# A mixture-of-experts layer: slot inversion by DRAM scatters instead of TensorE, an earlier slot computation, sigmoids placed by a table, first expert's tokens mixed in halves

## What is computed

```python
xk = x + (xprev - x) * time_maa_k
xr = x + (xprev - x) * time_maa_r
e_idx = token_ids.reshape(N) * 5099 % 16
pos = (rank of the token among those of its expert)
slot = where(pos < 512, e_idx * 512 + pos, 16 * 512)
expert_in = (xk placed by slot)                     # 16 x 512 x 512
h = square(relu(expert_in[e] @ w_key[e]))           # 512 -> 1024
expert_out = h @ w_value[e]                         # 1024 -> 512
y = expert_out[slot]                                # dropped: zero
out = x + sigmoid(xr @ w_recept.T) * y
```

## Time and profile before

| | us |
|---|---|
| median of 3 runs (lowest, highest) | 886.87 (886.42, 887.04) |
| the profiled execution, its own time | 886.9 |
| its span, first to last instruction | 885.2 |

### The profile page before, as it was taken

One profiled execution on the slowest core, in us unless ns is written; L12 is line 12 of the kernel. 1 busy time (PEld: TensorE's weight loads), 2 busy tenths in 40 slices (PEclk: granted clock), 3 DMA queues, 4 the chain that ended last, 5 costly groups with the idle time before them and its releaser, 6 DMA issues.

```text
span 885.2 us, 10910 instructions
## 1 busy us (share of the span) xinstructions
PE 877.8 (99%) x3920; PEld 723.8 (82%) x3920; DVE 733.0 (83%) x1020; ACT 412.7 (47%) x649; POOL 517.9 (59%) x468
## 2 busy tenths in 40 slices
PE   8999999999999999999999999999999999999997
PEld 6888888888888888888888888888888888888886
DVE  6787856869898989898989898989898988889862
ACT  7765557554444444444343434353535353535350
POOL 2000007677767676767676777677767776772411
PEclk9999999999999999999999999999999999999999
DMA  8765558775748484848484858575757675764521
GB/s 279 278 217 188 192 170 303 245 241 172 279 152 286 141 288 141 296 137 291 144 289 149 280 163 271 167 262 173 260 177 251 190 244 191 237 200 169 175 88 47
DMA packets 74054, 186.41 MB, mean 211 GB/s; under 512 B 11792, under 2 KB 12304, under 8 KB 74000
## 3 DMA queue, kind: packets, MB, share of 16 engines
q1 hardware_dynamic: 46064, 101.67, 35.8%
q0 software_dynamic: 27648, 83.91, 27.5%
q10 hardware_dynamic: 288, 0.13, 0.1%
HBM read 152.11 MB, written 33.55 MB: 210 GB/s over the span
## 4 chain that ended last, share of the span: by engine, by line
PE 98%; issue 1%; DMA 0%; DVE 0%; POOLq 0%; ACT 0%; POOL 0%; ACTq 0%
PE acc L869 32%; PE acc L871 32%; PE acc L870 32%; DMA wr_raw<-w_recept_t 0%; PE acc L885 0%; PE acc L889 0%; PE acc L893 0%; PE rt_bank L931 0%; POOLq L87 0%; POOL out L398 0%; DVE gate L765 0%; DVE xrow L768 0%; ACTq L495 0%; ACT wr_hi L501 0%; ACT xr_hi L507 0%
## 5 line engine op out<-in xcount | busy, mean ns | idle before, releaser
L391 POOL DMA_INDIRECT pair_even<-pairs,row_pair x128 | 140.3, 1096 | 164.2 <-DVE row_pair L704 125.5
L484 ACT ACTIVATE hid<-acc 128x512 f32<-128x512 f32 x128 | 76.6, 599 | 266.0 <-PE acc L871 266.0
L869 PE MATMUL acc<-xk_hi,wk_hi 128*128 128x512 f32 x512 | 199.5, 390 | 0.0
L871 PE MATMUL acc<-xk_hi,wk_lo 128*128 128x512 f32 x512 | 199.5, 390 | 0.0
L870 PE MATMUL acc<-wv_lo,h_hi 128*128 128x512 f32 x512 | 199.3, 389 | 0.0
L871 PE MATMUL acc<-wv_hi,h_lo 128*128 128x512 f32 x512 | 199.3, 389 | 0.0
L869 PE MATMUL acc<-wv_hi,h_hi 128*128 128x512 f32 x512 | 199.3, 389 | 0.0
L870 PE MATMUL acc<-xk_lo,wk_hi 128*128 128x512 f32 x512 | 199.2, 389 | 0.0
L391 POOL DMA_INDIRECT pair_odd<-pairs,row_pair x128 | 138.7, 1083 | 43.8 <-issue 38.7
L398 POOL DMA_INDIRECT out<-xrow,row_tok x64 | 85.7, 1339 | 113.3 <-DVE xrow L768 103.9
L753 DVE TENSOR_TENSOR hid<-hid 128x512 f32<-128x512 f32 x128 | 88.4, 691 | 53.0 <-ACT hid L484 51.3
(11 more groups left out here) (125 smaller groups left out, 1215.3 us busy)
## 6 DMA issues: line engine op xcount, KB each, us to landing
raw<-w_key SPq DMA_DIRECT2D x64, 512.0 KB, 4.6
raw<-w_value SPq DMA_DIRECT2D x64, 512.0 KB, 4.0
gates<-gate SPq DMA_DIRECT2D x64, 256.0 KB, 2.7
xT<-xs_t SPq DMA_DIRECT2D x63, 256.5 KB, 4.2
pair_even<-pairs,row_pair POOLq DMA_INDIRECT x128, 3.2
pair_odd<-pairs,row_pair POOLq DMA_INDIRECT x128, 3.1
xrow<-x,row_tok POOLq DMA_INDIRECT x64, 5.2
gate<-gates,row_tok POOLq DMA_INDIRECT x64, 4.5
```

What stands on the lines that cost most here:

```text
L391: pool.indirect_dma_start(pair[e % 2][:, i, :], None, pairs, bass.IndirectOffsetOnAxis(row_pair[:, a:a + 1], 0)).then_inc(s_pair[e % 2], 16)
L484: act.activation(hid[:, n % H_SLOTS, :], acc[n % 4][:, :], ACT.Relu).then_inc(s_relu, 1)
L869: pe.matmul(bank[:, :], hi, m_hi, start=first, stop=False)
L871: return pe.matmul(bank[:, :], lo, m_hi, start=False, stop=last)
```

## The change

It removes the one-hot matrices, `invert` and `spread`. Instead DVE computes for each token a place in DRAM (`place`); GpSimd waits for it and issues 64 indirect DMAs, each of which scatters 128 token numbers of 4 bytes into the DRAM list `slot_tok`, waits until all have landed, and issues 5 plain DMAs on its own queue: four that load the list, by lanes of 32, into `tok_q`, and one that loads `row_tok`. DVE makes `row_pair` from `tok_q` in round 52. The routing is now 14 pieces in rounds 1 to 19 and 52, its counts on TensorE come after steps 7 and 13, the token ids are loaded earlier on SP, and one strided reduction becomes a contiguous one with a strided write ahead of it. A table places the sigmoids. The first expert's tokens are mixed in 8 pieces of 256 columns in rounds 56 to 63, the first four of them from the first 8 gathers, the rest from the last 8. ACT's table load no longer waits for the identity matrix, which is gone.

```diff
-    PE_COUNT, PE_DROP, PE_INVERT, PE_SPREAD = 12, 22, 41, 44
-    DVE_ROUTE = (6, 8, 14, 16, 18, 19, 24, 25, 26, 28, 29, 30, 32, 33, 34, 36, 37, 42, 45)
-    FIRST_XK = (60, 61, 62, 63)
+    PE_COUNT, PE_DROP = 7, 13
+    DVE_ROUTE = (1, 3, 4, 5, 7, 8, 9, 10, 12, 13, 15, 16, 19, 52)
+    FIRST_XK = (56, 57, 58, 59, 60, 61, 62, 63)
     FIRST_KEY = (46, 49, 52, 55)
+    FIRST_TILE = (0, 1, 1, 1, 1, 2, 3)
+    LATE_TILES = 6
...
@@ sync
+                if k == 1:
+                    sp.dma_start(id_i, ids.rearrange("b (q j) -> (b q) j", j=J)).then_inc(s_ids, 16)
...
@@ gpsimd
+            pool.wait_ge(s_zero, 3)
+            pool.wait_ge(s_place, 1)
+            for j in range(J):
+                pool.indirect_dma_start(slot_tok, bass.IndirectOffsetOnAxis(place[:, j:j + 1], 0),
+                                        tok_id[:, j:j + 1], None).then_inc(s_put[j % 4], 16)
+            for i in range(4):
+                pool.wait_ge(s_put[i], 16 * J // 4)
+            for q in range(Q):
+                lanes = slice(q * BLOCK, (q + 1) * BLOCK)
+                pool.dma_start(tok_q[lanes, :].rearrange("r (b a) -> r b a", b=Q),
+                               slot_tok.rearrange("(b r a) o -> r b (a o)", b=Q, r=BLOCK)).then_inc(s_tok, 16)
+            pool.dma_start(row_tok[:, :], slot_tok.rearrange("(p a) o -> p (a o)", p=P)).then_inc(s_row_tok, 16)
             pool.wait_ge(s_rows, 1)
             gather_pairs(0)
+            pool.wait_ge(s_row_tok, 16)
...
@@ scalar
                 if n == 0:
-                    act.wait_ge(s_rows, 1)
+                    act.wait_ge(s_place, 1)
+            def split_first_xk(i):
+                half, k = divmod(i, KD)
+                cols = slice(half * HALF, (half + 1) * HALF)
+                act.wait_ge(s_first_xk, i + 1)
+                act.copy(xk_hi[:, k, cols], prev_t[:, k % 2, cols]).then_inc(s_first_xhi, 1)
...
-            act.wait_ge(s_ident, 1)
+            act.wait_ge(s_warm, 1)
...
+                    if g * KD + k in FIRST_XK:
+                        split_first_xk(FIRST_XK.index(g * KD + k))
-                    if k == min(g, KD - 1):
+                    if k == FIRST_TILE[min(g, len(FIRST_TILE) - 1)]:
                         sigmoids(g, (0,))
-                    if g < KD - 1 and k == g + 1:
+                    if g < LATE_TILES and k == FIRST_TILE[g] + 1:
                         sigmoids(g, (1, 2, 3))
-                    elif g >= KD and k == 0:
+                    elif g > LATE_TILES and k == 0:
                         sigmoids(g - 1, (1, 2, 3))
...
@@ vector, routing
+                step(dve.tensor_tensor(v["slot_drop"], v["slot_drop"], v["drop"], ALU.mult))
+                step(dve.tensor_tensor(v["slot_i"], v["slot_keep"], v["slot_drop"], ALU.add))
                 step(dve.tensor_scalar(v["a_i"], v["slot_i"], P.bit_length() - 1, None,
                                        ALU.logical_shift_right), False)
                 step(dve.tensor_scalar(v["b_i"], v["slot_i"], P - 1, None, ALU.bitwise_and))
+                dve.scalar_tensor_tensor(place[:, :], v["b_i"], A, v["a_i"], ALU.mult,
+                                         ALU.add).then_inc(s_place, 1)
...
+                dve.wait_ge(s_tok, 16 * Q)
                 dve.tensor_scalar(row_pair[:, :].rearrange("p (a b) -> p b a", b=Q),
+                                  tok_q[:, :].rearrange("p (b a) -> p b a", b=Q), float(Q),
                                   quarter[:, 0:1], ALU.mult, ALU.add).then_inc(s_rows, 1)
...
@@ vector, first expert
+            def mix_first_xk(i):
+                half, c = divmod(i, KD)
+                blocks, cols = slice(half * SB // 2, (half + 1) * SB // 2), slice(half * HALF, (half + 1) * HALF)
+                prev, cur = prev_t[:, c % 2, cols], cur_t[:, c % 2, cols]
+                if c == 0:
+                    dve.wait_ge(s_pair_first[half], 16 * SB // 2)
+                if c >= 2:
+                    dve.wait_ge(s_first_xlo, i - 1)
+                for part, dst in enumerate((prev, cur)):
+                    first = part * DQ + c * BLOCK
+                    dve.transpose(dst.rearrange("p (s r) -> p s r", r=BLOCK),
+                                  pair[0][:, blocks, first:first + BLOCK]).then_inc(s_first_block, 1)
+                dve.wait_ge(s_first_block, 2 * i + 2)
+                dve.tensor_tensor(prev, prev, cur, ALU.subtract).then_inc(s_first_diff, 1)
+                dve.wait_ge(s_first_diff, i + 1)
+                dve.scalar_tensor_tensor(prev, prev, maak[:, c:c + 1], cur,
+                                         ALU.mult, ALU.add).then_inc(s_first_xk, 1)
...
+                if r in FIRST_XK:
+                    i = FIRST_XK.index(r)
+                    if i == 0:
+                        dve.wait_ge(s_maak, 16)
+                    if i == KD:
+                        split_first_xk(i - 1)
+                    mix_first_xk(i)
+                    if i > 0 and i != KD:
+                        split_first_xk(i - 1)
+            split_first_xk(2 * KD - 1)
```

More of the change, by code:

```diff
@@ L103, in moe_token_shift @@
         sigmoid_table = sb("sigmoid_table", [P, 1], F32)
+        tok_id = sb("tok_id", [P, J], I32)
+        place = sb("place", [P, J], I32)
+        tok_q = sb("tok_q", [P, Q * A], I32)
+        lane_i = sb("lane_i", [P, 1], I32)
+        quarter_i = sb("quarter_i", [P, 1], I32)
+        quarter = sb("quarter", [P, 1], F32)
         mask = sb("mask", [P, A], F32)
@@ L203, in moe_token_shift @@
         drop_ps = rt_bank[:, 2 * E:2 * E + 1]
-        inv_ps = rt_bank[:, P:P + A]
-        tok_ps = rt_bank[:, 2 * P:2 * P + Q * A]
+        slot_tok = nc.dram_tensor("slot_tok", (N, 1), I32, kind="Internal").ap()
         s_ids = sem("s_ids")
@@ L222, in moe_token_shift @@
         s_pair = [sem(f"s_pair{b}") for b in range(2)]
+        s_pair_first = [sem(f"s_pair_first{h}") for h in range(2)]
         s_gat = [sem(f"s_gat{t}") for t in range(ST)]
@@ L234, in moe_token_shift @@
         s_count = sem("s_count")
-        s_oh = sem("s_oh")
-        s_inv = sem("s_inv")
+        s_place = sem("s_place")
+        s_row_tok = sem("s_row_tok")
+        s_put = [sem(f"s_put{i}") for i in range(4)]
         s_tok = sem("s_tok")
-        s_spread = sem("s_spread")
         s_rows = sem("s_rows")
@@ L251, in moe_token_shift @@
         s_wlo = sem("s_wlo")
+        s_first_block = sem("s_first_block")
+        s_first_diff = sem("s_first_diff")
+        s_first_xk = sem("s_first_xk")
+        s_first_xhi = sem("s_first_xhi")
+        s_first_xlo = sem("s_first_xlo")
         s_block = sem("s_block")
@@ L496, in _ @@
             act.dma_start(wr_raw[:, 0, 0:HALF], w_recept_t[0:P, 0:HALF]).then_inc(s_wr_half, 16)
-            act.wait_ge(s_ident, 1)
-            act.activation(sigmoid_table[:, :], ident[:, 0:1], ACT.Sigmoid)
+            act.wait_ge(s_warm, 1)
+            act.activation(sigmoid_table[:, :], warm[:, 0:1], ACT.Sigmoid)
             act.wait_ge(s_wr_half, 16)
@@ L578, in over, with residues @@
                 return w.unsqueeze(1).to_broadcast([P, n, w.shape[1]])
-            def by_group(w, n):
-                return w.rearrange("p (g i) -> p g i", i=JB).unsqueeze(2).to_broadcast(
-                    [P, w.shape[1] // JB, n, JB])
-            def each_group(w, n):
-                return w.unsqueeze(1).to_broadcast([P, n, w.shape[1], JB])
-            def by_slots(w):
-                return w[:, :, :].rearrange("p e j -> p j e")
-            def routing():
+            by_token = prod[:, :, :].rearrange("p e j -> p (e j)").rearrange("p (j e) -> p j e", e=E)
+            def residues():
                 dve.wait_ge(s_table, 1)
@@ L595, in routing @@
                 step(dve.tensor_copy(residue_b[:, :], residue[:, :]), False)
+            def routing():
                 dve.wait_ge(s_ids, 16)
@@ L625, in routing @@
                 yield
[L626 removed]
+                step(dve.tensor_reduce(v["slot_keep"], by_token, AX_X, ALU.add), False)
                 step(dve.tensor_tensor(empty_excl[:, :], empty_incl[:, :], empty[:, :], ALU.subtract))
@@ L635, in routing @@
                 dve.tensor_copy(drop_total[:, :], v["drop_cum"][:, J - 1:J]).then_inc(s_drops, 1)
-                step(dve.tensor_scalar(v["keep"], v["within"], float(C), None, ALU.is_lt), False)
+                yield
+                step(dve.tensor_scalar(v["keep"], v["within"], float(C), None, ALU.is_lt))
+                step(dve.tensor_tensor(v["slot_keep"], v["slot_keep"], v["keep"], ALU.mult), False)
                 yield
@@ L798, in _ @@
             route = routing()
+            residues()
             first_xr()
@@ L924, in count_drops @@
                           stop=True).then_inc(s_count, 1)
-            def invert():
-                pe.wait_ge(s_oh, 1)
-                for j in range(J):
-                    jg, i = divmod(j, JB)
-                    mm = pe.matmul(inv_ps[:, :], oh_b[:, jg, :, i], oh_aw[:, jg, :, i],
```

(12 more changed lines are left out.)

145 lines of the change are left out of this document (36 added, 109 removed).

## The result

The changed kernel takes 894.92 us (median of 6 runs, 893.57 to 895.68) against 886.88 before: a ratio of 1.0089, 95% interval 1.0079 to 1.0100. The forecast was 895.0, and the reason it gave is in the trace. The execution profiled took 894.86 us, its span 893.1.

What follows compares the result with a forecast made beforehand. TensorE, busy 99% of the span, was taken as the bound. 886.9 - 2.2 (removal) + 8.7 (wait in step 60) + 1.6 (slow clock) = 895.0 us, range 887.4 to 903.

Steps and rivals of the forecast that it cites:

- Removal: On TensorE: dropping `invert` and `spread` gains 2.2 us, all of it on the path.
- Loads: On POOL's queue behind the scatters: four plain list loads at 1.3 us each, the fourth landing at 151.4.
- First piece: On DVE in round 56: the first expert's first piece waits for the eighth gather, until 165.4 us.
- From the first piece to the sigmoid's end: On DVE and ACT, rounds 56 to 59: work and waits up to group 14's first sigmoid take 15.0 us, ending at 180.4.
- Wait: TensorE stands 8.6 us in the middle of step 60 for a sigmoid; the first expert comes 8.7 later.
- The eighth low half: On DVE: ends 23.0 us after the first piece's start, at 188.4, within TensorE's 189.3, so adds nothing.
- Clock: TensorE behind the standstill: the clock drops to 1.2 GHz and costs 1.6 us more.
- Afterwards: The second expert's pairs land by 204, DVE wants them at 204.9: covered by 1 us.
- 1 (later data): Wider scatter spacing makes the first expert's pairs much later: 902.7 us at 1.45, 915 at 1.64; chance 0.24.
- 2: Order alone: data there at 159.6, TensorE still waits 2.9 us, total 887.6; chance 0.08.
- 3: Not slower: group 14's first sigmoid is in time at 171.8, only the removal is left, 884.7 us; chance 0.08.
- 4: The clock stays up or data come at 163.0: 893.4 to 891.0 us; counted within the forecast's 0.60.

Runs made afterwards that it cites:

- experiment 6: Kernel before the change, without the 68 `invert` and `spread` matmuls, with fixed token lists made by iotas: 884.24 us, ratio 0.9969.
- after: The changed kernel itself, against the kernel before: 894.92 us, ratio 1.0089.
- experiment 2: Changed kernel with the first expert's eight pieces computed two per round in rounds 60 to 63 instead of one per round from 56: 890.09 us, ratio 1.0037.
- 8: As experiment 2, with the second expert's pair gathers ahead of the first expert's gathers of x rows on POOL: 885.63 us, ratio 0.9988.
- 10: As 8, with `row_pair` in round 51 and the first expert's key weight splits in rounds 46, 48, 50, 52: 885.80 us, ratio 0.9988.
- experiment 3: Changed kernel with 32 matmuls of zeros put on TensorE just before its wait in step 60: 892.63 us, ratio 1.0073.
- experiment 7: Changed kernel with eight more scatters, into a spare DRAM list, ahead of the wait for the landings: 904.29 us, ratio 1.0197.
- experiment 5: Changed kernel without scatters and loads, with fixed token lists, and `row_pair` in round 44 instead of 52: 889.38 us, ratio 1.0036.
- experiment 1: Changed kernel with ScalarE's sigmoids ahead of the copy for the first expert's piece in each round: 890.85 us, ratio 1.005.
- 4: Changed kernel without scatters and list loads, with fixed token lists made by iotas, `row_pair` still in round 52: 896.94 us, ratio 1.0115.

## Why the prediction was right, step by step

- **Removal**, 2.2: 2.3 from step 1 to step 60 in two kernels (experiment 6 and "after"). Step 60 came only 2.04 earlier, as step 1 itself started 0.26 later (the first four matmuls of step 0 took 1.75 for 1.16).
- **`place`** at 57.5: 57.3. **Spacing of scatters** 1.33: (139.82 - 58.23) / 63 = 1.295; 0.96 median and 0.30 between, what a gather costs.
- **Last landing** 3.0: 5.2 until POOL went on (the last scatter's own landing 4.5), a miss of 2.2. **Loads** 1.3 each: 0.58, a miss of 0.7 times three the other way by the fourth's start. Together with the faster scatters (1.5 earlier) the lists were there at about 149 (the fourth load at 146.8, landing 2.2 to 2.5 later), not at 151.4. `row_pair` ran at 150.16 instead of 151.4, held by its round and not by the lists. The prediction had that as its bound (150.1) and the lists as what decides; the order of the two was wrong, the size 1.2 us.
- **First piece** 165.4: 163.83; the first gather started 1.2 earlier, and the eighth landed in 2.85 for 3.5. The eighth gather came 10.1 behind the first for 9.8, since one took 2.09 beside the weight split.
- **From the first piece to the sigmoid's end** 15.0: 15.7. The operations took what was put down for them (0.40 to 0.48); VectorE's waits for ACT were 2.56, 0.76 and 0.66, 4.0 in all, for 3.2.
- **Wait** 8.6 (8.7 in the sum): 7.6 start to start over the usual distance (1.6 for earlier data, less 0.7 for a longer chain, and 0.2 for a later fourth tile). The place and the releaser were right.
- **The eighth low half** 23.0 behind the first piece's start: 24.2 (188.00), over the 0.9 that the prediction allowed. It cost nothing, because the pieces had started 1.6 earlier and TensorE reached the first expert at 190.85. This cover is the one that experiments 2, 8 and 10 ran into, with 1.0 to 1.2.
- **Clock** 1.6: 2.4. This is the term most mis-sized in proportion: it was taken from nine warm-up matmuls, and here twelve ran at 0.43. In the Trainium skill, "TensorE: Matmul & The Clock Gate", "Why this matters for your kernels" warns that a gap between bursts of matmuls sends the clock back to half; the 1.00 to 0.50 at 174.26 and experiment 3 agree with it.
- **Sum** 8.0 for 8.1: the errors of -1.1 in the wait, +0.8 in the clock and +0.2 in the earlier start of step 60 cancelled. That is luck: the time hit more closely than its parts deserve.
- **Cover of the early routing, the strided write, the earlier sigmoids**, at nothing: between steps 1 and 60 TensorE has no distance over 0.45 between two neighbours. Right.
- **Afterwards**, cover 1 us: it was some 6 (last pair gather of the second expert started at 197.69, wanted at 206.49, landing 3). Pessimistic, but it was the right place to look: in experiment 2 this cover was the one that went.
- **Rivals**: 1 (later data) fell by the spacing; with 9.4 us later data experiment 7 shows an earlier gap as its sign said, in step 56 instead of 57. 2 is experiment 5. 3 would have needed the 15.7 us of the chain in 8.1 (163.83 to 171.96). 4 held by half: the data came at 163.83, near its 163.0, but the clock fell. The scatters landed after 3.3 in the median and at most 5.0. In the Trainium skill, "DMA: Bandwidth & Descriptors", "Specifications" has transfers under 512 B read, modified and written back; the trace shows no cost of that in the spacing, and at most a part of the later last landing.

## What to carry over

When work is moved forward in an in-order queue, first write down what it waits for and what then stands behind it: the loss was a sigmoid that had its input, queued behind copies whose data came 18 us later than before. Removing a wait shows the next one, so follow every queue of the stage with the new dates before counting the whole wait as gain. A standstill of TensorE costs its length and, where the clock falls in it (7.87 and 4.83 us here, not 3.75), some 2 us more in the matmuls behind it.

## What was not expected of the hardware

- The clock and gaps of TensorE (start to start): 7.87, 4.83 (experiment 1) and 10.58 (4) brought the clock to 0.50, 3.75 (5), 3.45 (2) and 1.39 (8) did not. But in experiment 7 a gap of 3.32 did, and one of 2.51 was followed by a fall 0.7 us after matmuls had resumed. Length alone doesn't order these rows.
- GpSimd's indirect DMAs stretch beside VectorE's subtraction on 1024 columns: one gather of 0.95 became 2.1 in eight kernels. In experiment 7 both came 9 us later, together (163.55 and 163.58), and in 10 it was a scatter that stretched to 1.62. "Before" has it too: a gather of 1.63 at 151.48, beside the subtraction at 151.06. In the Trainium skill, "GPSIMD Engine Reference", "1. Specifications" has the two contend for SBUF access where a VectorE instruction has two SBUF inputs, as this one has; these rows agree. But the mixes and low halves on 512 columns have two such inputs as well, and the gather at 153.60 in "after" took 0.94 beside two of them (153.03 and 153.63), so two inputs alone don't make the stretch. Which property does was not tried.
- A scatter of 128 x 4 bytes costs GpSimd 0.96, about what a gather of 128 rows does (0.94 at least, 1.03 in the median); a plain DMA on its queue 0.55 to 0.64.
